# A CIN tower on one core: stream 1's first transfers move to ScalarE's queue, and gathers move ahead in GpSimd's

## The chip, the cores and the metric

The kernel runs on 1 core of one Trainium2 chip. Times are device microseconds (us) of one launch. A core has TensorE (PE in the profile), VectorE (DVE), ScalarE (ACT), GpSimd (POOL) and SyncE (SP, whose queue is SPq), and 16 DMA engines.

## The reference, cut to what matters

For each of 1024 samples, 32 rows of 16 numbers are looked up in 32 tables. Three layers multiply them with each other, and a small network follows.

```python
e = stack([tbl_f[ids[:, f]] for f in range(32)], axis=1)        # 1024 x 32 x 16
x0 = xk = e
for W in (W0, W1, W2):                                          # 32 x 32 x 64, then 32 x 64 x 64
    xk = relu(einsum('bmd,bhd,mhk->bkd', x0, xk, W))
    outs.append(sum(xk, axis=2))                                # 1024 x 64 each
h = concatenate([outs..., dense_ctx], axis=1)                   # 1024 x 208
h = maximum(h @ W_top1 + b_top1, 0); h = maximum(h @ W_top2 + b_top2, 0)
y = h @ W_top3
```

## The kernel before, in words

**Streams and tiles.** The 1024 samples are cut into 16 streams of 64. A stream's x0 has 64 x 16 = 1024 columns. Two streams, an even one (buffers a) and an odd one (b), make a tile, and the final network runs once per tile.

**Getting x0 in.** GpSimd looks up a stream's rows with 16 indirect DMAs (`gather`, L330), 256 in all, into `emb`, which has one half per stream of a tile. When a stream's 16 gathers have landed, SyncE stores `emb` twice to `x0_scratch` in HBM (`store_scratch`, L267), and then loads from there `base` (each field repeated on four partitions) and 16 chunks of `rolled` (`load_stream`, L285 and L294), 512 KB each: a chunk holds the fields turned by another number, so that all pairs of fields and maps come up. The first gather of stream i waits until stream i - 2 has been stored, since it overwrites its half of `emb`. SyncE goes through the streams one by one: the two stores, `base`, 16 chunks; for a stream above 1 each chunk waits until the stream two before has used its buffer.

**The layers.** A step is named (stream, layer, part). For each chunk an engine multiplies `rolled` with the layer's input, and TensorE multiplies the product with the chunk's weights and adds it up in `acc` (L591; in layer 0 also the squares, L600). The products are made by VectorE, two chunks at a time (`zd<-rolled`, L413, three buffers), and by GpSimd, one chunk at a time (`zg<-rolled`, L342, four buffers). VectorE reads the layer's input from PSUM (`xk_ps`), GpSimd from SBUF (`xk_sb`). Only in the very first step, (0,0,0), VectorE reads `base` from SBUF, chunk by chunk. At the end of layers 0 and 1 ScalarE copies `acc` with a ReLU to both inputs of the next layer (`evacuate`, L481), first `xk_sb`, then `xk_ps`, four halves each; only after (0,0) is part of the work done by VectorE (L422). At the start of a stream it copies `base` to `xk_ps` (L437) and squares it into `xk_sb` (L441).

**What sets the order.** `ORDER` lists the steps by hand: (0,0,0), (0,1,0), (1,0,0), (0,2,0), (1,1,0), (0,2,1), then tile by tile (1,2,0), (2,0,0), (1,2,1), (2,1,0), (3,0,0) and so on. `CHUNKS` says how many chunks of a step VectorE and GpSimd make. TensorE takes the products in the order of `merged`, VectorE's and GpSimd's interleaved.

**GpSimd's queue.** It holds gathers and products in one fixed order. `GATHERS_FIRST` gathers come first, then a wait for VectorE's first four products, then `GATHERS_EARLY` gathers; the two tables `GATHERS_AFTER` and `GATHERS_AFTER_AT` say how many gathers follow each product:

```python
gathers(GATHERS_FIRST)
pool.wait_ge(zd_ready, len(PLAN.dve[0]))
gathers(GATHERS_EARLY)
for q, (stream, layer, part) in enumerate(ORDER):
    ...
    for x, (_, n, j, _) in enumerate(PLAN.pool[q]):
        product(q, n, j)
        gathers(GATHERS_AFTER_AT.get(ORDER[q], GATHERS_AFTER.get((stream % 2, layer, part)))[x])
    gathers(GATHERS_MORE.get(ORDER[q], 0))
```

Of the kernel before, what the change touches and what calls it, by code (L numbers as in the profile page):

```python
# [15 lines left out]
FIELDS = 32  # L16
# [5 lines left out]
COLS = SAMPLES * DIM  # L22
# [7 lines left out]
GROUPS = P // FIELDS  # L30
GATHERS = SAMPLES // GROUPS
ROWS = 2 * FIELDS
NCH = FIELDS * MAPS // P
BASES = [1, 5, 9, 13, 0, 2, 3, 4, 6, 7, 8, 10, 11, 12, 14, 15]
L0CH = 4
# [4 lines left out]
ZD_BUFS = 3  # L40
ZG_BUFS = 4
# [10 lines left out]
for _t in range(1, TILES):  # L52
# [4 lines left out]
SUMS_AFTER = {0: 5, 1: 5, 2: 4}  # L57


GATHERS_FIRST = 24  # L60
GATHERS_EARLY = 8
GATHERS_AFTER = {(0, 1, 1): [3, 3], (1, 1, 0): [3, 3], (0, 2, 0): [3, 3, 2, 2], (1, 2, 0): [3], (1, 2, 1): [3, 4]}
GATHERS_AFTER_AT = {(0, 1, 0): [4, 7], (0, 2, 0): [3], (1, 1, 0): [3, 4], (0, 2, 1): [7],
                    (STREAMS - 1, 2, 0): [0, 0, 0, 0]}

GATHERS_MORE = {(2 * t, 1, 1): 3 for t in range(1, 6)}
# [34 lines left out]
PLAN = Plan()  # L101
# [50 lines left out]
def build_cin_tower(nc, ids, dense_t, tables, w0a, w0b, w12, wtop1, btop1, wtop2, btop2, wtop3, eye, out):  # L152
    with ExitStack() as ctx:
# [9 lines left out]
        rolled = sb("rolled", [P, 2, NCH, COLS])  # L163
# [86 lines left out]
        def bank_of(stream, layer):  # L250
            return 2 if layer == 0 else stream % 2

        def by_half(x):

            return x.rearrange("p (s h b) -> p s h b", s=2, h=2)
# [2 lines left out]
        last_h2_bank = [mlp[:, 0:TB], acc[:, 1, 0:TB]]  # L258
        last_y_bank = xk_ps[0:1, 0, 0:TB]

        @block.sync
        def _(sp):
            def store_scratch(i):

                sp.wait_ge(gathered[i % 2], 16 * GATHERS * (i // 2 + 1))
                for copy in range(2):
                    sp.dma_start(scratch[i, copy * FIELDS:(copy + 1) * FIELDS, :].rearrange(  # L267
                        "f (g c) -> (f g) c", g=GROUPS), emb[:, i % 2, :]).then_inc(scratch_in[i % 2], 16)

            def rows_from(first, i, step):  # L270
                return bass.AP(scratch.tensor, scratch.offset + (i * ROWS + first) * COLS,
                               [[COLS, FIELDS], [step * COLS, GROUPS], [1, COLS]])

            def load_stream(i):
                s = i % 2

                sp.wait_ge(scratch_in[s], 32 * (i // 2 + 1))
                if i > 0:

                    if i == 1:  # L280
                        sp.wait_ge(zd_ready, len(PLAN.dve[0]))
                    else:
                        sp.wait_ge(base_ps, 2 * (i - 1))
                    sp.wait_ge(squares_ready, i)
                sp.dma_start(base[:, :], rows_from(0, i, 0)).then_inc(base_in, 16)  # L285
                user = (i - 2, 2) if i > 1 else (i, 1)
                items = [x for q in range(len(ORDER)) if ORDER[q][:2] == user for x in PLAN.merged[q]]

                for who, n, first, w in sorted(items, key=lambda item: item[2] >= L0CH):
                    if i > 1:  # L290

                        sp.wait_ge(zd_ready if who == "dve" else zg_ready, n + 1)
                    for j in range(first, first + w):
                        sp.dma_start(rolled[:, s, j, :], rows_from(BASES[j], i, 1)).then_inc(rolled_in[s][j], 16)  # L294

            sp.dma_start(ids_sb[:, 0:1 + GATHERS], ids[:, 0:1 + GATHERS]).then_inc(first_ids_in, 16)
            sp.dma_start(ids_sb[:, 1 + GATHERS:], ids[:, 1 + GATHERS:]).then_inc(later_ids_in, 16)
            sp.dma_start(w0[:, :, :], w0a).then_inc(w0_in, 16)
            sp.dma_start(w0rev, w0b).then_inc(w0_in, 16)
            sp.dma_start(w12_sb[:, 0, :, :], w12[0]).then_inc(const_in, 16)  # L300
            sp.dma_start(w12_sb[:, 1, :, :], w12[1]).then_inc(const_in, 16)
            sp.dma_start(eye_sb[:, :], eye).then_inc(const_in, 16)
            sp.dma_start(wt1a[:, :], wtop1[0:P, :]).then_inc(const_in, 16)
            sp.dma_start(wt1b[:, :], wtop1[P:P + ZD_ROWS, :]).then_inc(const_in, 16)
            sp.dma_start(wt2[:, :, :], wtop2.rearrange("(c p) n -> p c n", p=P)).then_inc(const_in, 16)
            sp.dma_start(wt3[:, :], wtop3).then_inc(const_in, 16)
            sp.dma_start(bt1[:, :], btop1).then_inc(const_in, 16)
            sp.dma_start(bt2[:, :], btop2).then_inc(const_in, 16)
            sp.dma_start(z2d[MAPS:ZD_ROWS, :], dense_t).then_inc(const_in, 16)

            for i in range(STREAMS):
                store_scratch(i)
                load_stream(i)


            sp.wait_ge(y_ready, TILES)
            sp.dma_start(out.rearrange("b o -> o b"), y_sb[:, :]).then_inc(out_done, 16)
            sp.wait_ge(out_done, 16)
# [50 lines left out]
        def _(dve):  # L369
# [24 lines left out]
            for q, (stream, layer, _) in enumerate(ORDER):  # L394
                s = stream % 2
                if q == 0:

                    dve.wait_ge(base_in, 16)
                elif layer == 0:

                    dve.wait_ge(base_ps, 2 * stream)
                else:

                    dve.wait_ge(xk_ps_ready, 4 * evacuations(*phase_before(stream, layer)))
                for x, (_, n, j, w) in enumerate(PLAN.dve[q]):
                    if n >= ZD_BUFS:

                        dve.wait_ge(zd_used, n - ZD_BUFS + 1)
                    for c in range(j, j + w):
                        if layer == 0 or (layer == 1 and c >= L0CH):  # L410
                            dve.wait_ge(rolled_in[s][c], 16 * (stream // 2 + 1))
                    layer_in = base[:, :] if q == 0 else xk_ps[:, s, :]
                    nc.vector.tensor_tensor(zd[:, n % ZD_BUFS, 0:w, :], rolled[:, s, j:j + w, :],  # L413
                                            repeated(layer_in, w), ALU.mult).then_inc(zd_ready, 1)
                    for r in sums:
                        if sums[r] == (q, x):
                            reduce_d(r)
                if q == 0:

                    dve.wait_ge(zd_used, len(PLAN.dve[0]))  # L420
                    for copy in range(2):
                        nc.vector.tensor_scalar_max(xk_ps[copy * MAPS:(copy + 1) * MAPS, s, HALF:],  # L422
                                                    acc[MAPS:P, bank_of(0, 0), :], 0.0).then_inc(xk_ps_ready, 1)
# [5 lines left out]
        def _(act):  # L429
# [86 lines left out]
            act.wait_ge(base_in, 16)  # L516
            squares(0)
            evacuate(0, 0)
            base_to_ps(1)
            squares(1)  # L520
            evacuate(0, 1)
# [49 lines left out]
        def _(pe):  # L571
            def phase(q, between={}):
# [12 lines left out]
                for i, (who, n, j, w) in enumerate(merged):  # L585
                    pe.wait_ge(zd_ready if who == "dve" else zg_ready, n + 1)
                    for c in range(w):
                        weights = w0[:, j + c, :] if layer == 0 else w12_sb[:, layer - 1, j + c, :]
                        z = zd[:, n % ZD_BUFS, c, :] if who == "dve" else zg[:, n % ZG_BUFS, :]
                        for h in range(2):  # L590
                            end = nc.tensor.matmul(acc[h * MAPS:(h + 1) * MAPS, bank, :], weights,  # L591
                                                   z[:, h * HALF:(h + 1) * HALF],
# [154 lines left out]
```

## Time and profile before

| | |
|---|---|
| median of 3 runs | 616.87 us (615.1 to 616.98) |
| the profiled execution's own time | 617.09 us |
| its span in the profile | 615.3 us |
| TensorE busy | 562.9 us, 91% |
| VectorE busy | 553.3 us, 90% |
| GpSimd busy | 451.6 us, 73% |
| ScalarE busy | 366.7 us, 60% |
| DMA | 152.07 MB, mean 247 GB/s |
| chain that ended last | PE 74%, DVE 10%, DMA 6% |

The profile describes one execution. Busy time is the time in which an engine's instructions ran; a row's idle time stands in square brackets, with what ended it. The chain follows the last instruction back to what released it, step by step.

### The profile page before, as it was taken

The numbers are of one execution on the slowest core, as the hardware profiler recorded it, in microseconds if no ns is written. First come the engines' busy times: TensorE is split into PE (matmuls) and PEld (weight loads), VectorE is DVE, ScalarE is ACT, GpSimd is POOL, SyncE is SP. The second block draws the span as 40 slices with busy tenths as digits, with TensorE's granted clock in tenths as the row PEclk, the third lists the DMA queues.
The fourth block names the chain that finished last, engine by engine and source line by source line (L and its number), as shares of the span: only waits on it lengthen the run. The fifth ranks groups of instructions, "written<-read, shape, count | busy, mean of one in ns | idle before, by whom it ended". The sixth has DMA issues, their size and how long they took to land.

```text
span 615.3 us, 9070 instructions
## 1 busy us (share of the span) xinstructions
PE 562.9 (91%) x2752; PEld 209.7 (34%) x2752; DVE 553.3 (90%) x274; ACT 366.7 (60%) x2248; POOL 451.6 (73%) x347
## 2 busy tenths in 40 slices
PE   0049889999999999999999999999999999999997
PEld 0012222323333343334333333334333343334334
DVE  0058799999999999999999999999999999999990
ACT  0031606573867468774867468774868468674851
POOL 6748788878888788888888788888878864225430
PEclk9998899999999999999999999999999999999999
DMA  6297969793598819894598819794598809891000
GB/s 171 78 381 247 395 224 393 257 399 111 184 387 289 325 36 385 293 399 136 180 390 276 334 39 382 277 400 154 181 390 321 320 6 388 294 411 49 1 2 0
DMA packets 54259, 152.07 MB, mean 247 GB/s; under 512 B 9697, under 2 KB 18913, under 8 KB 54210
## 3 DMA queue, kind: packets, MB, share of 16 engines
q1 hardware_dynamic: 46018, 149.39, 64.6%
q0 software_dynamic: 8192, 2.11, 3.0%
q8 instruction: 21, 0.34, 0.2%
q14 instruction: 28, 0.23, 0.1%
HBM read 147.26 MB, written 4.20 MB: 246 GB/s over the span
## 4 chain that ended last, share of the span: by engine, by line
PE 74%; DVE 10%; DMA 6%; issue 4%; POOL 3%; SPq 1%; ACT 1%; DVEq 0%; POOLq 0%
PE acc L591 66%; DVE zd L413 10%; DMA rolled<-x_scratch 4%; POOL emb L330 3%; PE mlp L635 2%; PE acc L600 2%; PE mlp L626 1%; DMA emb<-tables_in,index 1%; PE mlp L627 1%; SPq L294 1%; DMA x_scratch<-emb 1%; PE mlp L607 1%; PE mlp L642 1%; ACT xk_sb L481 0%; ACT xk_ps L481 0%
## 5 line engine op out<-in xcount | busy, mean ns | idle before, releaser
L413 DVE TENSOR_TENSOR zd<-rolled,xk_ps 128x2048 f32<-128x2048 f32 (+1 forms) x246 | 536.1, 2254 | 11.6 <-DMA rolled<-x_scratch 5.3
L591 PE MATMUL acc<-zd,w_sb 128*64 128x512 f32 x1700 | 389.2, 596 | 8.9 <-DVE zd L413 8.8
L330 POOL DMA_INDIRECT emb<-tables_in,index x256 | 244.3, 954 | 79.6 <-issue 65.3
L342 POOL TENSOR_TENSOR zg<-rolled,xk_sb 128x1024 f32<-128x1024 f32 x87 | 207.1, 2383 | 59.3 <-ACT xk_sb L481 36.9
L591 PEld LDWEIGHTS acc<-zd,w_sb 128*64 128x64 f32 x1700 | 124.8, 137 | 250.2 <-issue 213.9
L460 ACT ACTIVATE relu_ab<-acc 128x16 f32<-128x16 f32 x928 | 153.7, 305 | 3.7 <-PE acc L591 3.5
L460 ACT ACTIVATION_READ_ACCUMULATOR relu_ab<-acc 128x1 f32 x928 | 154.3, 332 | 0.0
L481 ACT ACTIVATE xk_sb<-acc 64x512 f32<-64x512 f32 x128 | 75.8, 592 | 70.1 <-PE acc L591 67.5
L591 PE MATMUL acc<-zd,w 128*64 128x512 f32 x256 | 63.7, 618 | 38.6 <-DVE zd L413 38.6
L591 PE MATMUL acc<-zg,w_sb 128*64 128x512 f32 x348 | 90.7, 594 | 1.4 <-POOL zg L342 1.4
L481 ACT ACTIVATE xk_ps<-acc 64x512 f32<-64x512 f32 x126 | 71.8, 570 | 30.4 <-PE acc L591 27.6
L441 ACT ACTIVATE xk_sb<-base 128x1024 f32<-128x1024 f32 x16 | 16.9, 1057 | 57.0 <-PE acc L591 28.6
L591 PEld LDWEIGHTS acc<-zd,w 128*64 128x64 f32 x256 | 18.9, 142 | 74.2 <-issue 71.3
L591 PEld LDWEIGHTS acc<-zg,w_sb 128*64 128x64 f32 x348 | 25.3, 137 | 46.2 <-issue 42.9
L413 DVE TENSOR_TENSOR zd<-rolled,base 128x1024 f32<-128x1024 f32 x4 | 4.8, 1225 | 28.1 <-DMA rolled<-x_scratch 28.1
L437 ACT COPY xk_ps<-base 128x512 f32<-128x512 f32 x30 | 16.6, 587 | 22.3 <-DMA base<-x_scratch 17.8
L503 ACT ACTIVATE h<-mlp,bt 128x128 f32<-128x128 f32 x28 | 8.0, 368 | 23.8 <-PE mlp L627 23.8
L389 DVE TENSOR_REDUCE zpart<-relu_ab 128x32 f32<-128x512 f32 x19 | 13.0, 682 | 7.0 <-ACT relu_ab L493 7.0
L600 PE MATMUL acc<-xk_sb,w 128*64 128x512 f32 x64 | 18.4, 650 | 0.0
L497 ACT COPY z<-mlp 128x128 f32<-128x128 f32 x7 | 1.9, 266 | 24.0 <-PE mlp L607 20.6
L493 ACT ACTIVATE relu_ab<-acc 128x512 f32<-128x512 f32 x19 | 11.4, 598 | 7.5 <-PE acc L591 7.0
L635 PEld LDWEIGHTS mlp<-h,wt 128*128 128x128 f32 x112 | 13.0, 191 | 5.7 <-issue 5.7
(45 smaller groups left out, 102.5 us busy)
## 6 DMA issues: line engine op xcount, KB each, us to landing
rolled<-x_scratch SPq DMA_DIRECT2D x256, 512.0 KB, 10.3
base<-x_scratch SPq DMA_DIRECT2D x16, 512.0 KB, 3.7
emb<-tables_in,index POOLq DMA_INDIRECT x256
x_scratch<-emb SPq DMA_DIRECT2D x32, 128.0 KB
w_sb<-w_in SPq DMA_DIRECT2D x2, 512.0 KB, 5.0
wt<-wtop_in SPq DMA_DIRECT2D x1, 512.0 KB, 6.9
wt1a<-wtop_in SPq DMA_DIRECT2D x1, 256.0 KB, 5.8
w<-w0a_in SPq DMA_DIRECT2D x1, 160.0 KB, 2.3
```

What stands on the lines that cost most here:

```text
L330: pool.indirect_dma_start(emb[:, i % 2, c * DIM:(c + 1) * DIM], None, tables, bass.IndirectOffsetOnAxis(index[:, g:g + 1].bitcast(U32), 0) ...
L342: nc.gpsimd.tensor_tensor(zg[:, n % ZG_BUFS, :], rolled[:, s, j, :], xk_sb[:, s, :], ALU.mult).then_inc(zg_ready, 1)
L389: nc.vector.tensor_reduce(zpart[:, t % 2, layer, s, :], relu_ab[:, s, :].rearrange("p (b d) -> p b d", d=DIM), AX_X, ALU.add).then_inc(red ...
L413: nc.vector.tensor_tensor(zd[:, n % ZD_BUFS, 0:w, :], rolled[:, s, j:j + w, :], repeated(layer_in, w), ALU.mult).then_inc(zd_ready, 1)
L437: nc.scalar.copy(xk_ps[:, s, h * HALF:(h + 1) * HALF], base[:, h * HALF:(h + 1) * HALF]).then_inc(base_ps, 1)
L441: nc.scalar.activation(xk_sb[:, i % 2, :], base[:, :], ACT.Square).then_inc(squares_ready, 1)
L460: end = nc.scalar.activation(relu_ab[:, s, cols], acc[:, bank, cols], ACT.Relu, accum_out=zpart[:, t % 2, layer, s, b:b + 1])
L481: nc.scalar.activation(dst[copy * MAPS:(copy + 1) * MAPS, s, h * HALF:(h + 1) * HALF], acc[h * MAPS:(h + 1) * MAPS, bank, :], ACT.Relu).th ...
L493: nc.scalar.activation(relu_ab[:, s, :], acc[:, bank, :], ACT.Relu).then_inc(relu_ready, 1)
L591: end = nc.tensor.matmul(acc[h * MAPS:(h + 1) * MAPS, bank, :], weights, z[:, h * HALF:(h + 1) * HALF], start=(j + c == 0), stop=(i == len ...
L600: nc.tensor.matmul(acc[h * MAPS:(h + 1) * MAPS, bank, :], w0[:, L0CH, :], xk_sb[:, s, h * HALF:(h + 1) * HALF], start=False, stop=False)
L635: end = nc.tensor.matmul(mlp[:, c * TB:(c + 1) * TB], wt2[:, k, c * P:(c + 1) * P], h1[:, k, :], start=(k == 0), stop=(k == H1 // P - 1))
```

## The change

- The first tile's `GATHERS_FIRST` goes from 24 to 28 and `GATHERS_EARLY` from 8 to 4.
- The gathers behind GpSimd's first six products go from 4, 7, 3, 3, 4, 7 to 3, 2, 8, 5, 6, 8, four more in all, so that from there on every gather stands four places further ahead among the products.
- Stream 1's two stores, its `base` and its chunks 0 to 3 are issued by ScalarE, behind its evacuation of (0,0) and ahead of `base_to_ps(1)`, `squares(1)` and its evacuation of (0,1). SyncE keeps chunks 4 to 15 of stream 1, which wait for the same two stores.
- The first four products of VectorE go to both halves of two `zd` buffers, one chunk in each, and the wait for TensorE ahead of the fourth of them is gone.

```diff
-GATHERS_FIRST = 24
-GATHERS_EARLY = 8
+GATHERS_FIRST = 28
+GATHERS_EARLY = 4
...
-GATHERS_AFTER_AT = {(0, 1, 0): [4, 7], (0, 2, 0): [3], (1, 1, 0): [3, 4], (0, 2, 1): [7],
+GATHERS_AFTER_AT = {(0, 1, 0): [3, 2], (0, 2, 0): [8], (1, 1, 0): [5, 6], (0, 2, 1): [8],
...
+        def zd_of(q, n, w):
+
+            return zd[:, n // 2, n % 2:n % 2 + 1, :] if q == 0 else zd[:, n % ZD_BUFS, 0:w, :]
+
...
+        def load_chunk(engine, i, j):
+            engine.dma_start(rolled[:, i % 2, j, :], rows_from(BASES[j], i, 1)).then_inc(rolled_in[i % 2][j], 16)
...
-                sp.dma_start(base[:, :], rows_from(0, i, 0)).then_inc(base_in, 16)
+                if i != 1:
+                    sp.dma_start(base[:, :], rows_from(0, i, 0)).then_inc(base_in, 16)
...
-                        sp.dma_start(rolled[:, s, j, :], rows_from(BASES[j], i, 1)).then_inc(rolled_in[s][j], 16)
+                        if i != 1 or j >= L0CH:
+                            load_chunk(sp, i, j)
...
-                store_scratch(i)
+                if i != 1:
+                    store_scratch(sp, i)
...
-                    if n >= ZD_BUFS:
+                    if q > 0:
...
             evacuate(0, 0)
+
+            store_scratch(act, 1)
+            act.wait_ge(scratch_in[1], 32)
+
+            act.wait_ge(zd_ready, len(PLAN.dve[0]))
+            act.dma_start(base[:, :], rows_from(0, 1, 0)).then_inc(base_in, 16)
+            for j in range(L0CH):
+                load_chunk(act, 1, j)
             base_to_ps(1)
             squares(1)
             evacuate(0, 1)
```

GpSimd's queue from the start, before: gathers (`emb<-`) and products (`zg<-`), down to the product of (1,2,0), which is the seventh.

```order
L330 DMA emb<-tables_in,index 128x16 x32
...
L342 TENSOR_TENSOR zg<-rolled,xk_sb 128x1024
L330 DMA emb<-tables_in,index 128x16 x4
L342 TENSOR_TENSOR zg<-rolled,xk_sb 128x1024
L330 DMA emb<-tables_in,index 128x16 x7
L342 TENSOR_TENSOR zg<-rolled,xk_sb 128x1024
L330 DMA emb<-tables_in,index 128x16 x3
...
L330 DMA emb<-tables_in,index 128x16 x4
L342 TENSOR_TENSOR zg<-rolled,xk_sb 128x1024
L330 DMA emb<-tables_in,index 128x16 x7
```

The same piece now, with all six products and their gathers.

```order
L336 DMA emb<-tables_in,index 128x16 x32
...
L348 TENSOR_TENSOR zg<-rolled,xk_sb 128x1024
L336 DMA emb<-tables_in,index 128x16 x3
L348 TENSOR_TENSOR zg<-rolled,xk_sb 128x1024
L336 DMA emb<-tables_in,index 128x16 x2
L348 TENSOR_TENSOR zg<-rolled,xk_sb 128x1024
L336 DMA emb<-tables_in,index 128x16 x8
L348 TENSOR_TENSOR zg<-rolled,xk_sb 128x1024
L336 DMA emb<-tables_in,index 128x16 x5
L348 TENSOR_TENSOR zg<-rolled,xk_sb 128x1024
L336 DMA emb<-tables_in,index 128x16 x6
L348 TENSOR_TENSOR zg<-rolled,xk_sb 128x1024
L336 DMA emb<-tables_in,index 128x16 x8
```

The gathers are spread differently, and the seventh product stands behind 64 of them instead of 60.

ScalarE's queue now, from its evacuation of (0,0) to the one of (0,1).

```order
L499 ACTIVATE relu_ab<-acc 128x512
L273 DMA x_scratch<-emb 128x256 x2
L530 DMA base<-x_scratch 128x1x1024
L277 DMA rolled<-x_scratch 128x1x1024 x4
L443 COPY xk_ps<-base 128x512 x2
L447 ACTIVATE xk_sb<-base 128x1024
L487 ACTIVATE xk_sb<-acc 64x512 x4
L487 ACTIVATE xk_ps<-acc 64x512 x4
```

The three rows of DMAs are new there. On SyncE the row of stream 0's loads now reads x28 and runs on into stream 1's chunks 4 to 15.

## Rows read from the trace of the kernel before

**Rows 1.** Busy time by stretch: engines, then clock, DMA share, GB/s.

```profile
106.00:156.00 50.00, 47.71 (x230) 16.19 (x228) 49.85 (x26) 29.67 (x169) 41.89 (x33) 1.00 0.70 249
160.00:325.00 165.00, 165.00 (x816) 61.70 (x814) 163.90 (x80) 116.10 (x759) 142.28 (x109) 1.00 0.76 280
470.00:600.00 130.00, 130.00 (x662) 50.99 (x658) 127.39 (x61) 87.89 (x599) 65.64 (x35) 1.00 0.51 195
```

The engine columns are PE, PEld, DVE, ACT and POOL, each with its number of instructions.

**Rows 2.** Chain of waits, 20 to 90 us: start, length, what.

```profile
47.83 5.21 DMA emb<-tables_in,index
...
53.42 2.20 DMA x_scratch<-emb
...
56.84 6.77 DMA rolled<-x_scratch
```

**Rows 3.** Timeline of VectorE: start, length, operation, idle time before and what ended it.

```profile
55.07 4.48 DVE L413 TENSOR_TENSOR zd<-rolled,xk_ps 128x2048 f32<-128x2048 f32 x2
63.74 2.29 DVE L413 TENSOR_TENSOR zd<-rolled,xk_ps 128x2048 f32<-128x2048 f32 x1 [4.18 <-DMA rolled<-x_scratch]
66.49 8.88 DVE L413 TENSOR_TENSOR zd<-rolled,xk_ps 128x2048 f32<-128x2048 f32 x4 [0.47 <-DMA rolled<-x_scratch]
...
77.27 4.49 DVE L413 TENSOR_TENSOR zd<-rolled,xk_ps 128x2048 f32<-128x2048 f32 x2 [1.29 <-ACT xk_ps L481]
...
104.83 13.28 DVE L413 TENSOR_TENSOR zd<-rolled,xk_ps 128x2048 f32<-128x2048 f32 x6
```

**Rows 4.** Timeline of GpSimd: the gather after its stop, and four products.

```profile
39.09 0.94 POOL L330 DMA_INDIRECT emb<-tables_in,index  x1 [6.10 <-DVE zd L413]
...
48.87 2.39 POOL L342 TENSOR_TENSOR zg<-rolled,xk_sb 128x1024 f32<-128x1024 f32 x1
...
56.17 2.37 POOL L342 TENSOR_TENSOR zg<-rolled,xk_sb 128x1024 f32<-128x1024 f32 x1
...
67.18 2.37 POOL L342 TENSOR_TENSOR zg<-rolled,xk_sb 128x1024 f32<-128x1024 f32 x1
...
99.28 2.40 POOL L342 TENSOR_TENSOR zg<-rolled,xk_sb 128x1024 f32<-128x1024 f32 x1
```

**Rows 5.** Timeline of ScalarE, 59 to 68 us.

```profile
59.71 1.11 ACT L437 COPY xk_ps<-base 128x512 f32<-128x512 f32 x2 [13.56 <-DMA base<-x_scratch]
...
63.15 2.44 ACT L481 ACTIVATE xk_sb<-acc 64x512 f32<-64x512 f32 x4 [1.35 <-PE acc L591]
65.61 2.35 ACT L481 ACTIVATE xk_ps<-acc 64x512 f32<-64x512 f32 x4
```

**Rows 6.** Timeline of TensorE: its waits near 60 us, and step (1,2,0).

```profile
58.59 1.08 PE L591 MATMUL acc<-zg,w_sb 128*64 128x512 f32 x4 [1.41 <-POOL zg L342]
...
66.17 2.48 PE L591 MATMUL acc<-zd,w 128*64 128x512 f32 x8 [3.07 <-DVE zd L413]
...
104.47 1.94 PE L591 MATMUL acc<-zd,w_sb 128*64 128x512 f32 x8 [0.35 <-DVE zd L413]
106.21 1.06 PE L591 MATMUL acc<-zg,w_sb 128*64 128x512 f32 x4
```

**Rows 7.** Busy time by stretch around the second wait of rows 6.

```profile
64.00:68.00 4.00, 1.83 (x8) 0.87 (x10) 3.53 (x2) 3.83 (x8) 3.37 (x4) 0.93 1.03 400
68.00:72.00 4.00, 4.00 (x14) 1.42 (x12) 4.00 (x3) 0.59 (x1) 3.48 (x3) 0.65 1.04 395
```

**Rows 8.** Timelines of SyncE, GpSimd and TensorE, 449 to 469 us.

```profile
449.05 1.08 SPq L267 DMA_DIRECT2D x_scratch<-emb  x2
...
453.98 2.40 POOL L342 TENSOR_TENSOR zg<-rolled,xk_sb 128x1024 f32<-128x1024 f32 x1
...
462.39 0.94 POOL L330 DMA_INDIRECT emb<-tables_in,index  x1 [3.62 <-DMA x_scratch<-emb]
463.34 2.40 POOL L342 TENSOR_TENSOR zg<-rolled,xk_sb 128x1024 f32<-128x1024 f32 x1
...
463.84 1.03 PE L591 MATMUL acc<-zg,w_sb 128*64 128x512 f32 x4
...
468.13 1.03 PE L591 MATMUL acc<-zg,w_sb 128*64 128x512 f32 x4
```

More of the change, by code:

```diff
@@ L259, in build_cin_tower, with rows_from, store_scratch @@
         last_y_bank = xk_ps[0:1, 0, 0:TB]
+        def rows_from(first, i, step):
+            return bass.AP(scratch.tensor, scratch.offset + (i * ROWS + first) * COLS,
+                           [[COLS, FIELDS], [step * COLS, GROUPS], [1, COLS]])
+        def store_scratch(engine, i):
+            engine.wait_ge(gathered[i % 2], 16 * GATHERS * (i // 2 + 1))
+            for copy in range(2):
+                engine.dma_start(scratch[i, copy * FIELDS:(copy + 1) * FIELDS, :].rearrange(
+                    "f (g c) -> (f g) c", g=GROUPS), emb[:, i % 2, :]).then_inc(scratch_in[i % 2], 16)
+        def load_chunk(engine, i, j):
+            engine.dma_start(rolled[:, i % 2, j, :], rows_from(BASES[j], i, 1)).then_inc(rolled_in[i % 2][j], 16)
         @block.sync
         def _(sp):
[L263 to L272, printed above, removed]
-            def load_stream(i):
[L275 to L283, printed above, removed]
+            def load_stream(i):
+                sp.wait_ge(scratch_in[i % 2], 32 * (i // 2 + 1))
+                if i > 1:
+                    sp.wait_ge(base_ps, 2 * (i - 1))
                     sp.wait_ge(squares_ready, i)
-                sp.dma_start(base[:, :], rows_from(0, i, 0)).then_inc(base_in, 16)
+                if i != 1:
+                    sp.dma_start(base[:, :], rows_from(0, i, 0)).then_inc(base_in, 16)
                 user = (i - 2, 2) if i > 1 else (i, 1)
@@ L412, in _ @@
                     layer_in = base[:, :] if q == 0 else xk_ps[:, s, :]
-                    nc.vector.tensor_tensor(zd[:, n % ZD_BUFS, 0:w, :], rolled[:, s, j:j + w, :],
+                    nc.vector.tensor_tensor(zd_of(q, n, w), rolled[:, s, j:j + w, :],
                                             repeated(layer_in, w), ALU.mult).then_inc(zd_ready, 1)
@@ L588, in phase @@
                         weights = w0[:, j + c, :] if layer == 0 else w12_sb[:, layer - 1, j + c, :]
-                        z = zd[:, n % ZD_BUFS, c, :] if who == "dve" else zg[:, n % ZG_BUFS, :]
+                        z = zd_of(q, n, w)[:, c, :] if who == "dve" else zg[:, n % ZG_BUFS, :]
                         for h in range(2):
```

## The prediction, made before the changed kernel was run

> **What bounds the kernel now.** I read four views in this order: busy time by stretch, the chain of waits, the timelines of the engines in the first 110 us, and those around 450 us.
>
> Busy time by stretch splits the run in three [rows 1]. From 160 us on TensorE has no idle time: 165.00 of 165 us, 130.00 of 130 us between 470 and 600. Whatever makes it wait there lengthens the run by as much. Between 106 and 156 us VectorE is busy 49.85 of 50 us and TensorE 47.71: VectorE sets the pace, and TensorE could take back some 2.3 us. Ahead of that lie the waits that the change is aimed at. The chain has them one behind the other [rows 2]: stream 1's last gather, issued at 47.83 and landed 5.21 us later, its store (2.20), and the loads that land at 63.61. VectorE pays 4.18 us at 63.74, 0.47 at 66.49 and 1.29 at 77.27 [rows 3], 5.9 us in all: the most that the change can win.
>
> **The front, stream 1.** The four gathers that move ahead of GpSimd's stop fit into its 6.10 us of idle time [rows 4]. After the stop four remain, so the last is issued at 39.09 + 3 x 1.25 = 42.84 instead of 47.83 and lands at 48.05 if it takes 5.21 again. ScalarE then issues the store. If that lands as before, 2.58 us after the gather, it is there at 50.6; if it takes the 5.21 of the gather beside the loads of stream 0, at 53.3; before, at 55.62. From there VectorE's first product of stream 1 came 8.1 us later, its second 10.9 later, the base's copy on ScalarE 4.1 [rows 3, 5]. What the trace of before doesn't show is two queues loading at once: SyncE issues stream 1's other 12 chunks from the same semaphore on. Lower bound: they cost nothing. Upper bound: they take half of the rate, so base, chunk 0 and 1 need 3 x 1.3 us more and chunks 2 and 3 another 2 x 1.3 (512 KB at the 395 GB/s of a loaded stretch is 1.3 us [rows 7]). The first product starts at 58.7 to 65.3, the second at 61.5 to 70.7, against 63.74 and 66.49. The gathers, which suffered beside loads (5.21 us), are the nearest row, so I take sharing, with the early store: 62.6 and 68.0.
>
> The Trainium skill, "DMA: Bandwidth & Descriptors", section "Issuing engines are not separate DMA queues", says that transfers issued by different engines run on the same 16 DMA engines and interleave, and that only the sequencer's issue time is saved. By that rule the split gains nothing in bandwidth and takes some from the first chunks; the trace of before has no two such queues to show it.
>
> A second limit stands behind the loads. VectorE's next phase, (0,2,0), reads xk_ps of (0,1). Its last product for (0,1) ends at 59.55 [rows 3], TensorE takes 1.94 for a pair of chunks [rows 6], and ScalarE copies xk_sb in 2.44 and then xk_ps in 2.35 [rows 5]: 61.6, 64.1, 66.4. The 1.41 us that TensorE waits for GpSimd's second product [rows 6] go, since that product starts earlier, and this is included. So (0,2,0) starts at 66.4 at best and at 73.0 at worst, before at 68.7; with my values at 70.2. Three products and a sum (7.3 us: before 68.7 to 77.27 less the wait of 1.29) bring (1,1,0) to 73.7, 80.3 or 77.5; before it began at 77.27. **The front is worth -3.6 to +3.0 us to VectorE; I take 0.** ScalarE waits for the base in between; even at 50.6 + 4.1 + 1.3 = 56.0, or 53.3 + 5.4 = 58.7, it has 2.2 us of copying to do before 61.6, so that costs nothing as long as the base has landed by 59.4.
>
> The second buffer half for the first four products (the removed wait) is worth nothing: they wait for their chunks, not for TensorE. Their cover is the loading of stream 0.
>
> **GpSimd, where the price is.** From product to product it takes 7.30 us with 4 gathers between (48.87 to 56.17) and 11.01 with 7 (56.17 to 67.18) [rows 4]: 2.35 + 1.24 per gather. Before, the gathers behind its first six products were 4, 7, 3, 3, 4, 7; now 3, 2, 8, 5, 6, 8. The first two of these fall in a time where it then has to wait: its third product, of (0,2,0), needs xk_sb of (0,1), which is there at 64.1, as worked out. This was 67.18 before, behind seven gathers. From 64.1 on nothing lets GpSimd pause: 8 gathers, product at 76.4; 5, 84.9; 6, 94.7; 8, the product of (1,2,0) at 107.0, ended at 109.4. Each of these is behind its gathers alone: xk_sb of (1,0), the only other thing that one of them needs anew, is there by 75. Before it began at 99.28 and TensorE took it at 106.21 [rows 4, 6]. **TensorE has to wait there until 109.4, 3.2 us later than before**, however early VectorE is. VectorE has three buffers, so it goes on at first. The product of 104.83 is the next that TensorE takes, and its buffer serves the third one after it, which started at 104.83 + 3 x 2.2 = 111.4 [rows 3]. Now TensorE frees it after GpSimd's chunk and that pair of chunks (1.06 and 1.94, which overlap by 0.2 [rows 6]), at 109.4 + 2.8 = 112.2. So 0.8 us stay with VectorE, and the rest TensorE takes back by 156. But an idle TensorE loses its clock: after an idle time of 3.07 us the granted clock was 0.93 and then 0.65 over two stretches of 4 us [rows 6, 7], from 2.4 GHz to 1.2 GHz for part of them, a loss of 4 x 0.07 + 4 x 0.35 = 1.7 us. Here it idles for 3.2 us if VectorE is on time, more if it is early. So 0.8 to 2.5 (the drop delays the same buffer); the idle time lies close to the one that brought the drop, and I take a value between, 1.8.
>
> **The same queue, 340 us later.** Gather 240, stream 15's first, waits for the store of stream 13, whose buffer it overwrites. That store was issued at 449.05, behind 16 loads in SyncE's queue, and released GpSimd at 462.39 after 3.62 us of waiting [rows 8]. Gather 240 was the third behind the product of 453.98, and the product of 463.34 came right after. With all gathers four further on, gather 240 stands ahead of the product of 453.98, with one more gather between. Even 5 us late GpSimd reaches it before 459, so it waits for the store as before, and now the product of 453.98 stands behind it: 462.39 + 1.25 + 0.95 = 464.6, ended 467.0, where TensorE took it at 463.84: 3.1 us of waiting. The next product is due at 464.6 + 2.35 + 3 x 1.24 = 470.7, ended 473.1, taken at 468.13 before: 4.9 us in all, on top of the shift that the tile already has. TensorE has no idle time there to take it back [rows 1]. A clock drop at the first of the two waits only moves time from the second.
>
> **Sum.** 0 (front) + 1.8 + 4.9 = 6.7 us on the profiled execution's 617.09, that is 623.8; the median of the runs shown is 0.2 lower, so 623.6.
>
> **Rivals.**
> - *The second wait does not come* (12%): the store of stream 13 lands earlier relative to TensorE, or gather 240 is not behind it. Against it: the order of the queue and 3.62 us of waiting already there. Only 1.8 us are left: 618.7, on the edge of what counts as no change.
> - *The front gain gets through* (6%), the faster side. It decides at TensorE's wait at 106.21: if GpSimd's products of the first tile went out of its queue 4 us sooner than 2.35 + 1.24 per gather allows, so that the one of (1,2,0) ended by 105, the 3.6 us would stay: 613.3. It needs the wait at 462.39 to be harmless as well.
> - *ScalarE is held* (10%). Its store, base and loads stand ahead of its evacuation of (0,1). If the base lands at 63 instead of by 59.4, xk_sb, GpSimd's third product and all behind it slip by 3.6: 627.2.
> - *The early gathers and the first products collide* (8%). Four gathers now run beside VectorE's first four products, which read two SBUF tensors; before, GpSimd stood still there. If each held a product up for its 0.94 us, everything slips by 3.8: 627.4. The Trainium skill, "SBUF — State Buffer", section "SBUF: two separate sides", says that GpSimd and a VectorE instruction with two SBUF inputs lock each other out of a shared port pair; no row of before has the two together.
>
> **Chances.** Forecast 64%, rivals 12, 6, 10 and 8%. A measurement can tell 0.3% (1.85 us) from no change: faster than 615.0 has 6%, within it 11%, slower 83%. The range reaches from the first rival (618.6) to just over the dearest (628.0); it leaves out the faster side and sums of two misfortunes.
>
> **What would show it.** In the profile after, GpSimd's product of (1,2,0) should end near 109.4, and TensorE should show a wait for it of 2 to 6 us, against none before. Near 465 to 473 us (plus 2) there should be two waits of TensorE for zg, with GpSimd waiting for x_scratch a product earlier. VectorE's waits of 4.18 and 1.29 should be smaller or moved. It is wrong if TensorE never waits for zg past 100 us, if the third GpSimd product starts before 63, or if stream 1's base lands after 60.

## The result, and the profile after

The changed kernel takes 624.75 us (median of 6 runs, 623.83 to 627.11), the kernel before, in turn with it on the same chip, 616.65 (6 runs, 614.52 to 617.14). The ratio is 1.0135, with a 95% interval from 1.0105 to 1.0164: 8.1 us slower, with 6.5 to 10.1 as the interval. The forecast was 623.6, the range 618.6 to 628.0.

TensorE after 100 us first. The waits by engine, of the changed kernel, TensorE's rows (engine, line, operand, releaser: us in total, times, longest):

```profile
PE acc L605 <- DVE zd L419: 50.0, 18, 35.5
PE acc L605 <- POOL zg L348: 5.5, 5, 1.6
```

Five waits for GpSimd's product (zg), 5.5 us. Past 100 us the kernel before had none. Their places are in the timeline of TensorE, changed kernel:

```profile
110.81 1.08 PE L605 MATMUL acc<-zg,w_sb 128*64 128x512 f32 x4 [1.34 <-POOL zg L348]
...
449.66 1.03 PE L605 MATMUL acc<-zg,w_sb 128*64 128x512 f32 x4
450.52 1.89 PE L605 MATMUL acc<-zd,w_sb 128*64 128x512 f32 x8
453.97 1.08 PE L605 MATMUL acc<-zg,w_sb 128*64 128x512 f32 x4 [1.56 <-POOL zg L348]
...
458.77 1.08 PE L605 MATMUL acc<-zg,w_sb 128*64 128x512 f32 x4 [0.28 <-POOL zg L348]
...
470.06 1.08 PE L605 MATMUL acc<-zg,w_sb 128*64 128x512 f32 x4 [0.78 <-POOL zg L348]
...
476.09 1.08 PE L605 MATMUL acc<-zg,w_sb 128*64 128x512 f32 x4 [1.51 <-POOL zg L348]
```

The chunks that TensorE took at 106.21, 463.84 and 468.13 [rows 6, 8] it now takes at 110.81, 470.06 and 476.09. The shift is 4.60 at the first and 7.96 at the last. Two more chunks, matched by their place in the order of steps, tell when it grows: the one taken at 157.24 before is taken at 160.30, the one at 446.68 at 449.66. So the shift is 3.0 us at 160 and still 3.0 at 450; the rest of the first 4.60 was taken back. **The 8 us are two losses: 3.0 that are there by 160, and 5.0 between 449.66 and 476.09.**

The first loss starts at VectorE. Its timeline, changed kernel:

```profile
55.98 4.47 DVE L419 TENSOR_TENSOR zd<-rolled,xk_ps 128x2048 f32<-128x2048 f32 x2
65.83 2.29 DVE L419 TENSOR_TENSOR zd<-rolled,xk_ps 128x2048 f32<-128x2048 f32 x1 [5.38 <-DMA rolled<-x_scratch]
70.95 8.88 DVE L419 TENSOR_TENSOR zd<-rolled,xk_ps 128x2048 f32<-128x2048 f32 x4 [2.83 <-DMA rolled<-x_scratch]
...
80.35 4.47 DVE L419 TENSOR_TENSOR zd<-rolled,xk_ps 128x2048 f32<-128x2048 f32 x2
```

The wait of 1.29 us for xk_ps before (1,1,0) [rows 3] is gone, but those for the loads have grown from 4.18 and 0.47 to 5.38 and 2.83, and (1,1,0) begins at 80.35 instead of 77.27: 3.1 us late. ScalarE's timeline says when these loads could start:

```profile
48.88 0.83 ACTq L273 DMA_DIRECT2D x_scratch<-emb  x2
54.80 0.60 ACTq L530 DMA_DIRECT2D base<-x_scratch  x1
55.43 2.91 ACTq L277 DMA_DIRECT2D rolled<-x_scratch  x4
60.36 1.11 ACT L443 COPY xk_ps<-base 128x512 f32<-128x512 f32 x2 [13.32 <-DMA base<-x_scratch]
61.41 1.05 ACT L447 ACTIVATE xk_sb<-base 128x1024 f32<-128x1024 f32 x1
62.49 2.44 ACT L487 ACTIVATE xk_sb<-acc 64x512 f32<-64x512 f32 x4
```

The store is issued at 48.88, and the base, which waits for it, at 54.80: 5.9 us. It was issued 4.2 us earlier than before and landed only 0.8 earlier, at 54.78 against 55.62. Until shortly before that stream 0's loads fill the DMA engines (386 to 403 GB/s from 40 to 52 us). From 54.80 two queues load. By the landings in the trace ScalarE's chunks 0 to 3 come at 63.15, 65.71, 68.27 and 70.83, each 2.56 us after the other, with a chunk of SyncE's between each two (65.39, 67.95, 70.51). Before, chunks 0 to 3 came at 61.97, 63.61, 64.89 and 66.37, 1.3 to 1.6 us apart.

GpSimd's timeline, changed kernel, first tile:

```profile
33.12 0.94 POOL L336 DMA_INDIRECT emb<-tables_in,index  x1 [0.30 <-issue]
34.36 1.82 POOL L336 DMA_INDIRECT emb<-tables_in,index  x1 [0.30 <-issue]
36.48 1.02 POOL L336 DMA_INDIRECT emb<-tables_in,index  x1 [0.30 <-issue]
37.81 1.12 POOL L336 DMA_INDIRECT emb<-tables_in,index  x1 [0.30 <-issue]
39.76 0.94 POOL L336 DMA_INDIRECT emb<-tables_in,index  x1 [0.83 <-DVE zd L419]
...
65.00 2.35 POOL L348 TENSOR_TENSOR zg<-rolled,xk_sb 128x1024 f32<-128x1024 f32 x1 [7.72 <-ACT xk_sb L487]
...
108.38 2.37 POOL L348 TENSOR_TENSOR zg<-rolled,xk_sb 128x1024 f32<-128x1024 f32 x1
```

The third product is early (65.00, before 67.18), the one of (1,2,0) late (108.38, before 99.28). The 27 gathers between them are the cause, with one wait of 0.58 us at 77.79, for the xk_sb of (1,0), which ScalarE had ready at 77.72.

Around 460 us, GpSimd's timeline of the changed kernel:

```profile
456.31 2.40 POOL L348 TENSOR_TENSOR zg<-rolled,xk_sb 128x1024 f32<-128x1024 f32 x1
458.87 0.98 POOL L336 DMA_INDIRECT emb<-tables_in,index  x1 [0.16 <-issue]
465.43 0.94 POOL L336 DMA_INDIRECT emb<-tables_in,index  x1 [5.58 <-DMA x_scratch<-emb]
466.67 0.94 POOL L336 DMA_INDIRECT emb<-tables_in,index  x1 [0.30 <-issue]
467.64 2.37 POOL L348 TENSOR_TENSOR zg<-rolled,xk_sb 128x1024 f32<-128x1024 f32 x1
...
473.67 2.36 POOL L348 TENSOR_TENSOR zg<-rolled,xk_sb 128x1024 f32<-128x1024 f32 x1
```

Gather 240 is held at the store of stream 13 for 5.58 us (before 3.62 [rows 8]); this wait is called the hold from here on. It ends at 465.43, and behind gather 240 comes one more gather before the product of 467.64.

### The profile page after: what moved, and what is told of

The parts are those of the page before. It is cut to its first block, busy times and chain, and to the rows that moved or that the text cites. A ratio compares the mean times of both kernels' runs of the same rounds, so it can differ in the third digit from the quotient of the medians.

```text
span 623.2 us, 9069 instructions
## 1 busy us (share of the span) xinstructions
PE 564.2 (91%) x2752; PEld 207.8 (33%) x2752; DVE 553.9 (89%) x274; ACT 365.7 (59%) x2248; POOL 452.7 (73%) x347
## 4 chain that ended last, share of the span: by engine, by line
PE 63%; POOL 19%; issue 8%; DMA 5%; DVE 3%; SPq 1%; ACT 1%; DVEq 0%; POOLq 0%
PE acc L605 56%; POOL emb L336 13%; POOL zg L348 7%; DMA rolled<-x_scratch 2%; DMA x_scratch<-emb 2%; DVE zd L419 2%; PE mlp L649 2%; PE acc L614 2%; PE mlp L640 1%; PE mlp L641 1%; SPq L277 1%; PE mlp L656 1%; PE mlp L621 1%; DMA emb<-tables_in,index 0%; ACT xk_sb L487 0%
```

## The experiments

Theory A, from the two traces: the change has two independent costs. The queue split brings the front in 3 to 4 us late, and the four gathers that GpSimd is ahead move the hold at gather 240 in front of a product, for 5. GpSimd's late product of (1,2,0) is a third limit, hidden while VectorE is late itself. Rival B: one cause, GpSimd's gathers, makes all of it, and the front is only jitter. Rival C: the queue split costs by itself whatever the loads do (ScalarE's issues ahead of its copies). Each experiment's recorded expectation stands ahead of its result and may name further rivals. Differences are taken against the kernel before as timed beside each (616.46 for the first four, 616.06 for the next four).

**1. The queue alone.** The change with the gather numbers of before:

```diff
-GATHERS_FIRST = 28
-GATHERS_EARLY = 4
+GATHERS_FIRST = 24
+GATHERS_EARLY = 8
-GATHERS_AFTER_AT = {(0, 1, 0): [3, 2], (0, 2, 0): [8], (1, 1, 0): [5, 6], (0, 2, 1): [8],
+GATHERS_AFTER_AT = {(0, 1, 0): [4, 7], (0, 2, 0): [3], (1, 1, 0): [3, 4], (0, 2, 1): [7],
```

> The queue part alone: ScalarE issues stream 1's stores, base and first four chunks, GpSimd's order of gathers is the one before the change. Theory A (two separate costs: 3 us because two queues share the engines at stream 1's first chunks, and 5 us because gather 240 stands ahead of the product that TensorE takes at 464; together 8): the store lands near 55.6, chunks 2 and 3 then need 16 us as after the change, so VectorE's step (1,1,0) starts near 81 instead of 77.3 and the kernel is 3 to 4 us slower than before, 620 to 621, with no wait of TensorE for zg near 465. Theory B (all comes from GpSimd being four gathers late): no change, 616.7. Theory C (ScalarE is held by its transfers): its evacuation of (0,1) starts later than 63.2 and the cost grows with it.

Measured 620.25 us, ratio 1.0065 [1.0049, 1.0082]: 3.8 us slower. VectorE, this kernel:

```profile
65.36 2.29 DVE L419 TENSOR_TENSOR zd<-rolled,xk_ps 128x2048 f32<-128x2048 f32 x1 [7.46 <-DMA rolled<-x_scratch]
70.86 8.88 DVE L419 TENSOR_TENSOR zd<-rolled,xk_ps 128x2048 f32<-128x2048 f32 x4 [3.22 <-DMA rolled<-x_scratch]
...
80.26 4.47 DVE L419 TENSOR_TENSOR zd<-rolled,xk_ps 128x2048 f32<-128x2048 f32 x2
```

These are the starts of the change itself within 0.5 us, with GpSimd's gathers as before. B falls. The run also holds the new `zd` halves of the first four products, which no run has alone; in the trace of before the fourth of them waited only for its chunk (0.19 us, at 37.60), not for TensorE.

**2. The gathers alone.** The kernel before, all loads on SyncE, with the change's gather numbers (28 and 4; [3, 2], [8], [5, 6], [8]).

> The gathers part alone, all of stream 1's transfers on SyncE as before. Theory A: no sharing of two queues, so VectorE's step (1,1,0) starts 1 to 2 us earlier than before (75 to 76), but GpSimd's product of (1,2,0) ends near 110.7 whatever VectorE does, TensorE waits for it by 3 us or more, and 2 to 4 us stay; near 465 the same 5 us as after the change. 624 to 626, as slow as the whole change. Theory B agrees. Theory D (the sharing of the queues is the cause of the front's 3 us and GpSimd's lateness there costs nothing): only the 5 us near 465 less what the front gains, 620 to 621.

Measured 623.29 us, ratio 1.0129 [1.0096, 1.0162]: 6.8 slower, a little less than expected. (1,1,0) begins at 75.47, 1.8 earlier than before, and TensorE waits 2.81 us for the product of (1,2,0). At the chunk of 157.24 1.1 of the 1.8 are left, and at the one of 446.68, taken at 445.79 here, 0.9; between them lies one more wait for GpSimd, 0.29 us at 176.38. The waits near 450 to 472 are there as in the change: from that chunk to the one of 468.13 it is 26.66 us. By the medians the two halves alone cost 3.8 + 6.8 = 10.6 and together 8.1. That is no proof of an overlap: the interval of this run reaches from 5.9 to 10.0 us (its four times from 621.53 to 626.93), and the traces, read at the chunk of 468.13, give 2.3 (experiment 1), 4.3 (this run, its fastest execution) and 8.0 (the change).

**3. The hold moved back.** The change with three gathers fewer behind step (10,1,1), in the tile of streams 10 and 11. Gather 240 then stands one place ahead of where it stood before the change, not four, and behind the same product as there:

```diff
-GATHERS_MORE = {(2 * t, 1, 1): 3 for t in range(1, 6)}
+GATHERS_MORE = {(2 * t, 1, 1): 3 for t in range(1, 5)}
```

> The changed kernel with three gathers fewer in tile 5 (behind stream 10's second part of layer 1), so that gather 240 stands behind the product that TensorE takes at 464 to 467 and not ahead of it. Theory A: the two waits of TensorE for zg near 467 and 473 are gone and so are the small ones ahead of them; 5 us less than the change, 619.5 to 620.5. Theory B' (GpSimd as a whole is the bound by then, and the hold only shows it): it stays within 1 us of the change, 624.

Measured 619.75 us, ratio 1.0047 [1.0030, 1.0064]. That is 3.3 us slower than before: three gathers less in one place give back 4.8 of the 8.1. TensorE and GpSimd, this kernel:

```profile
449.83 1.03 PE L605 MATMUL acc<-zg,w_sb 128*64 128x512 f32 x4
...
467.00 1.03 PE L605 MATMUL acc<-zg,w_sb 128*64 128x512 f32 x4
...
471.29 1.03 PE L605 MATMUL acc<-zg,w_sb 128*64 128x512 f32 x4
```

```profile
458.62 2.38 POOL L348 TENSOR_TENSOR zg<-rolled,xk_sb 128x1024 f32<-128x1024 f32 x1
...
465.62 0.94 POOL L336 DMA_INDIRECT emb<-tables_in,index  x1 [3.48 <-DMA x_scratch<-emb]
...
467.83 2.39 POOL L348 TENSOR_TENSOR zg<-rolled,xk_sb 128x1024 f32<-128x1024 f32 x1
```

The hold ends at the same time, 465.62 against 465.43, though SyncE issued the store that ends it 3.6 us earlier here (452.16 against 455.79). But the product of 458.62 is now ahead of it and TensorE takes that one at 467.00 without a wait. 449.83 to 471.29 is 21.46 us, as before the change (446.68 to 468.13, 21.45); in the change it is 26.43.

**4. The hold alone, in the kernel before.** One line, nothing else of the change. Gather 240 comes to stand three places further ahead, directly in front of a product:

```diff
+GATHERS_MORE[10, 1, 1] = 6
```

> The kernel before with three gathers more behind tile 5's second part of layer 1, so that gather 240 stands ahead of the product that TensorE takes at 464; nothing else. Theory A: the hold by the store of stream 13 costs alone what it costs in the change, TensorE waits near 464 and 468 for zg, 5 us in all, 621 to 622. Rival (the hold costs only with GpSimd already late from the first tile): under 1 us, 616.5 to 617.5.

Measured 620.50 us, ratio 1.0073 [1.0058, 1.0087]: 4.4 slower, somewhat under expectation. From 445.86 to 470.88 TensorE takes 25.02 us for what took 21.45, so this trace has 3.6 of it. GpSimd, this kernel:

```profile
461.47 0.94 POOL L331 DMA_INDIRECT emb<-tables_in,index  x1 [5.79 <-DMA x_scratch<-emb]
462.43 2.37 POOL L343 TENSOR_TENSOR zg<-rolled,xk_sb 128x1024 f32<-128x1024 f32 x1
...
468.46 2.37 POOL L343 TENSOR_TENSOR zg<-rolled,xk_sb 128x1024 f32<-128x1024 f32 x1
```

The hold alone makes the larger part of the change's loss in a kernel that is otherwise the one before. The change loses 1.4 more there, and its trace says why: the product for TensorE's last wait starts 8.24 us after the end of the hold (465.43 to 473.67), here 6.99 (461.47 to 468.46). The difference, 1.25, is the one gather more that four places instead of three put between them.

**5. SyncE lets ScalarE's loads go first.** The change, with SyncE's chunks 4 to 15 of stream 1 behind the landing of chunk 3:

```diff
                 if i != 1:
                     sp.dma_start(base[:, :], rows_from(0, i, 0)).then_inc(base_in, 16)
+                else:
+                    sp.wait_ge(rolled_in[1][L0CH - 1], 16)
```

> The changed kernel, but SyncE starts its 12 chunks of stream 1 only when ScalarE's four have landed. Theory A: with the engines to themselves chunks 2 and 3 land near 65 instead of 70.8, VectorE's (1,1,0) starts near 75 instead of 80.4; but GpSimd's product of (1,2,0) still ends near 110.7, TensorE waits for it 3 to 7 us, loses clock, and 2 to 4 us stay behind it. With the 5 us near 465 it comes out at 623 to 626, no better than the change. Theory D (sharing alone is the front's cost, GpSimd's lateness is harmless): 3 to 5.5 us less than the change, 619 to 621.5.

Measured 624.04 us, ratio 1.0129 [1.0098, 1.0160]: 7.6 slower, against 8.1 for the change. (1,1,0) begins at 75.38 instead of 80.35, so the 3 us of the front come from sharing the DMA engines, not from ScalarE's queue as such: C falls. And the median hardly moves. A part of the reason is in TensorE's timeline, this kernel:

```profile
107.75 1.08 PE L607 MATMUL acc<-zg,w_sb 128*64 128x512 f32 x4 [3.23 <-POOL zg L350]
108.66 3.28 PE L607 MATMUL acc<-zd,w_sb 128*64 128x512 f32 x8
```

GpSimd's late product takes over as the limit, and the clock drops. (1,1,0) began 1.9 us earlier than before, but the chunk of 446.68 is taken at 447.08, 0.4 later: this wait took 2.3 us, where the one of experiment 2, without a drop, took 0.9. From there to the chunk of 468.13 it is 26.50 us, so the hold is 5.05. That makes 5.5 us, and the trace does have 2.6 of the 3.0 us of the front back. The rest of the 7.6 it doesn't show: the four times fall in two pairs, 622.21 and 622.56, 625.52 and 625.77. The trace is of the execution at 622.56, 2.5 faster than the profiled one of the change (625.05); of the slower pair there is none.

**6. Gathers refitted.** The change with the numbers behind the first products set so that gather 240, and the product of (1,2,0), stand as before:

```diff
-GATHERS_AFTER_AT = {(0, 1, 0): [3, 2], (0, 2, 0): [8], (1, 1, 0): [5, 6], (0, 2, 1): [8],
+GATHERS_AFTER_AT = {(0, 1, 0): [3, 8], (0, 2, 0): [3], (1, 1, 0): [3, 4], (0, 2, 1): [7],
```

> The changed kernel's queues, but the gathers behind the six products 3, 8, 3, 3, 4, 7: 28 of them as before the change, eight of them in the time in which GpSimd waits for xk_sb of (0,1). Theory A: GpSimd's product of (1,2,0) ends near 98 to 100, TensorE waits for no zg after 60 us, nothing is lost near 465, and what is left is the sharing of the two queues at stream 1: VectorE's (1,1,0) near 80 as after the change, 3 to 4 us slower than before, 619.5 to 620.5. Rival (queues harmless, all of the cost in the gathers' order): 616 to 617.

Measured 620.40 us, ratio 1.0059 [1.0045, 1.0074]. TensorE has no wait for zg at all, so all GpSimd costs are gone, and 4.3 us stay: the shared loads, as in 1.

**7. Both.** Experiments 5 and 6 together.

> As the last, and SyncE holds its 12 chunks of stream 1 back until ScalarE's four have landed: no sharing, no late GpSimd, no hold ahead of the product. Theory A: both costs are gone. The front gives no more than 0.3 us, as the run with SyncE waiting showed (its store landed no earlier, behind the loads of stream 0). 616 to 617, no change from before. Rival (a third cost, such as ScalarE's transfers or the early gathers beside the first products, is still in it): 618 or more.

Measured 615.46 us (12 runs), ratio 0.9984 [0.9974, 0.9995]: 0.6 faster than the kernel before, and 9 faster than the change. With the two causes away, none of the 8 us is left. VectorE, this kernel:

```profile
62.03 9.12 DVE L421 TENSOR_TENSOR zd<-rolled,xk_ps 128x2048 f32<-128x2048 f32 x4 [3.19 <-DMA rolled<-x_scratch]
...
76.83 4.49 DVE L421 TENSOR_TENSOR zd<-rolled,xk_ps 128x2048 f32<-128x2048 f32 x2 [1.97 <-ACT xk_ps L489]
```

The first product comes 1.7 us earlier than before [rows 3], but (1,1,0) only 0.4: VectorE waits 0.84 us for TensorE at 71.98 and 1.97 for the copy into xk_ps, the next limit.

**8. The copies swapped.** Experiment 7, and ScalarE copies xk_ps ahead of xk_sb after (1,0):

```diff
-                    if (s, layer) != (0, 0):
+                    if (s, layer) != (0, 0) and (stream, layer) != (1, 0):
                         copies.reverse()
```

> As the run with refitted gathers and SyncE waiting, and ScalarE copies xk_ps before xk_sb after (1,0), since VectorE waits 1.3 to 1.5 us there for xk_ps while GpSimd's next product has over 9 us of slack. Theory A: VectorE's wait at its step (1,1,0) goes, 1.3 us less than that run, about 615.3. Rival (VectorE's lead is lost again before TensorE becomes the bound at 150 us, since GpSimd's products come 2.4 us later): no gain, 616.5.

Measured 614.60 us (8 runs, 613.39 to 618.31), ratio 0.9983 [0.9966, 0.9999]. VectorE, this kernel:

```profile
64.13 8.88 DVE L421 TENSOR_TENSOR zd<-rolled,xk_ps 128x2048 f32<-128x2048 f32 x4 [0.35 <-DMA rolled<-x_scratch]
...
73.52 4.47 DVE L421 TENSOR_TENSOR zd<-rolled,xk_ps 128x2048 f32<-128x2048 f32 x2
```

The wait is gone and (1,1,0) begins 3.8 us earlier than before. It is the fastest median of the study, 1.5 us under the kernel before, with an interval that just stays below 1. Whether it beats experiment 7 these runs do not say.

**9 and 10. The first wait alone; one queue.** Two questions were left: what the late product of (1,2,0) costs without the hold (experiment 5 with the line of experiment 3), and whether the best version needs ScalarE's queue at all (the kernel before with 28 and 4, [3, 8], [3], [3, 4], [7] and the copies swapped). Each ran in two series.

> The changed kernel with both other costs taken out: SyncE waits for ScalarE's four chunks, and tile 5 has three gathers fewer. What is left is GpSimd's lateness in the first tile, 64 gathers ahead of its product of (1,2,0). Theory A: that product ends near 107.7, TensorE waits 2.8 to 3.3 us for it and 1.8 to 2.6 us stay: 618 to 619. Rival (a wait of TensorE in a stretch paced by VectorE is taken back whole): 615.5 to 616.5.

> The kernel before, with 28 gathers ahead of the stop, 3 and 8 behind the first two products, and xk_ps copied before xk_sb after (1,0); all transfers on SyncE. Theory A (ScalarE's queue gives nothing, since the store waits for the loads of stream 0 in whichever queue it stands): as fast as the run with the copies swapped, 614.6, within 0.5 us. Rival (the second queue brings the store earlier and this is where the gain of the last two runs came from): 616 or more.

> The same kernel as in the run of the first wait alone, whose step (0,1) began 7 us late (at 50.1) beside a before whose runs spread over 6 us. Theory (the late product of (1,2,0) is a floor of its own, worth some 2 us when the front is on time): step (0,1) begins near 42 to 43.5, VectorE's (1,1,0) at 75.5, TensorE waits about 3.2 us for zg near 105 to 108, no wait for zg near 450 to 475; 618 to 619, ratio to before 1.003 to 1.004. Rival (the two floors are one and the same loss, so that without the second the first costs nothing): 616. Second rival (the late step belongs to this kernel and not to its surroundings): step (0,1) again at 50, some 5 us over before.

> The same kernel as in the run of one queue with the earlier gathers and the copies swapped, whose step (0,1) also began at 50.0. Theory (the second queue has no part in the gain of the best version: it comes from the gathers ahead of GpSimd's stop and from xk_ps being copied first): step (0,1) near 42 to 43.5, VectorE's (1,1,0) near 73.5, no wait for zg past 100 us, 614.6, ratio 0.997 to 0.999. Rival (ScalarE's queue gives a part of it): 615.5 to 616, ratio 0.999 to 1.000. Second rival (the late step belongs to this kernel): step (0,1) again at 50, some 5 us over before.

Measured: the first wait alone 627.40 and 627.43 us (ratios 1.0105 [1.0058, 1.0153] and 1.0148 [1.0086, 1.0211]); one queue 626.37 and 624.54 (1.0084 [1.0042, 1.0126] and 1.0101 [1.0073, 1.0128]). All are far off, and not by a mechanism that the first two expectations asked about; the last two name it as their second rival. ScalarE, in the first of them:

```profile
48.60 1.17 ACT L489 ACTIVATE xk_ps<-acc 64x512 f32<-64x512 f32 x2 [17.53 <-remote]
```

In all four profiles the first evacuation, (0,0), starts between 48.28 and 48.60 us, where the change has it at 42.9 and the other kernels between 39.4 and 42.5. TensorE, VectorE and ScalarE stand still from 44 to 48, while the DMA engines go on, and TensorE's granted clock is 0.50 in the stretch after. TensorE's last matmuls were issued by 41 in all of them; what held their results isn't in the trace. SyncE is late as well: it issues the last chunk of stream 0 between 43.3 and 44.2 us, in the other kernels between 37.0 and 38.2.

The second rival of the last two expectations, that the late step belongs to these kernels, came about as far as it can be seen: (0,1) began at 49.76 and 49.88 again, and the two kernels were 9.6 and 6.8 us over before. Each run of the new kernels is over 621. But the kernel of the first wait alone does the same as that of experiment 5 until step (10,1,1), near 415 us, and there (0,1) began at 41.86, so the order of its work up to there isn't enough to cause it. And in these two series the kernel before itself spread over 614.6 to 623.3 us, which it did in no other, so the surroundings have a part. The cause stays open, and with it both questions. What the first wait costs is known only from what it leaves of an earlier front: 0.9 in the trace of experiment 2 and 2.3 in that of experiment 5.

## Why the prediction was right

Right in direction, in size (1.2 us off, inside the range) and in its largest term. One term was wrong by +3.1, and one of 1.8 was added where it should not have been. That the two offset each other in part was luck: the total is off by less than either of these terms.

- **The front, taken as 0: wrong, it was +3.1**, the upper end that the prediction worked out (80.3; measured 80.35). The step that failed is "I take sharing, with the early store". Sharing came. The early store did not: it landed 5.9 us after its issue, not the 2.58 that were taken, and more than the 5.21 of the bound (53.3; measured 54.78). Its nearest row was the gather beside the loads of stream 0, which the prediction had in hand and used only as a bound. With it the sum had been right for the front, though by two errors that cancel: the store was 1.5 us later than the bound, and from it to the first two products it took 11.05 and 16.17 us, 2.9 and 5.3 more than before, where half of the rate was worked out as 3.9 and 6.5.
- **The rule of the Trainium skill** ("DMA: Bandwidth & Descriptors", "Issuing engines are not separate DMA queues") speaks of transfers of two issuers interleaving on the same 16 DMA engines. The trace agrees: 2.56 us per chunk of 512 KB on ScalarE's queue beside SyncE's, against 1.3 to 1.6 alone, one of each in turn.
- **The product of (1,2,0): right in place, its cost hidden.** It was to end at 109.4 and ended at 110.75: GpSimd's third product began at 65.00 and not at 64.1, and at 77.79 it waited 0.58 us for the xk_sb of (1,0), which the prediction had "there by 75" and which the late front moved to 77.72. TensorE waited 1.34 us for it and not 3.2: VectorE was late itself. The 1.8 us of the sum were not there: the shift, 3.1 at the chunk before it (99.55), is 4.6 at 106.21 and 3.1 again at 137.03, and experiment 3 repeats it (3.0, 4.5, 3.0, with a wait of 1.36). With the front on time the waits were 2.81 us without a drop of the clock and 3.23 with one. They cost 0.7 and 2.7 us at the chunk of 157.24, 0.9 and 2.3 at the one of 446.68 (experiments 2 and 5; shifts drift by up to 0.7 between these two chunks with no wait for zg, as in experiment 1): about the two ends of the 0.8 to 2.5, each with the cause that the prediction gave for it. The slower executions of both kernels have no trace. What failed is the addition: the late front and the late product are two limits in parallel, the later one rules, and a front that is 3 us late doesn't pay for the product as well.
- **The hold at gather 240: right.** Taken 4.9; measured 4.98 in the trace (26.43 less 21.45), 4.8 by experiment 3, 5.2 and 5.05 in the traces of experiments 2 and 5, 3.6 in the kernel before with three places instead of four (experiment 4; 4.4 by its times), where the one gather fewer behind the hold makes 1.25 of the difference. The product that was to start at 464.6 and the next at 470.7, with the tile's shift of 3.0, started at 467.64 and 473.67. Only the waits lie differently: four of 0.28 to 1.56 us from 453.97 on, not two. The first two come from products that GpSimd made ahead of the hold, which holds it from 459.85 on: it was late there already. They add nothing to the 5.0, since the last product starts 8.24 us after the end of the hold in any case (the same in experiments 2 and 5).
- **The sum.** 0 + 1.8 + 4.9 = 6.7 forecast; 3.1 + 0 + 5.0 = 8.1 measured.
- **The rivals.** "The second wait does not come": it did. "The front gain gets through": there was none. "ScalarE is held": the base landed at 60.34, past the 59.4 set for it, and ScalarE's copy of (0,1) began at 62.49 instead of 61.6. No run shows that the base caused these 0.9 us: TensorE ended (0,1) at 62.44 and ScalarE its work on the base at 62.46, and (0,1) had begun 0.9 us later than before (44.38 against 43.48, in the traces of the eight other kernels that ran as expected 40.85 to 43.98). It cost nothing in the end. The late base was also on the list of what would make the prediction wrong ("lands after 60"): by that sign it should have been wrong, and what the sign tells of is the late store, the step that failed. "The early gathers and the first products collide": they do, but the other way round. The gathers took 1.82, 1.02 and 1.12 us instead of 0.94, while VectorE's products took 1.22 to 1.23 each, as before. GpSimd had 6 us to spare there, so it cost nothing. That agrees with the Trainium skill, "SBUF — State Buffer", "SBUF: two separate sides", as far as one locks out the other. The Trainium skill says there that whichever starts first has the shared ports for its whole instruction. The gather of 34.36, begun 0.22 us after a product, fits that; those of 36.48 and 37.81 began ahead of the products of 36.89 and 38.27, and still it was they that took longer.

## What to carry to other kernels

A second queue is no second path: issuing the urgent transfers there helps only if the others are held back meanwhile (5.0 us at the start of (1,1,0), from one wait on SyncE), and a store issued 4 to 5 us early lands only 0.8 to 1.8 us earlier while the DMA engines are full (54.78 in the change, 53.8 in experiments 2 and 5, 55.62 before). Where one engine does both background work and products in a fixed order, count where the background work can be held (here gather 240), and what stands right behind it: moving it by four places in the first tile cost 5 us some 400 us later, and one line takes them back. Limits that run in parallel are not added: work out when each would release the pacing engine, take the latest, and expect the next one to appear when it is removed.

## What the runs showed of the hardware

- **The clock after an idle time.** TensorE idled 2.81 us in experiment 2 and kept the upper of its two levels (2.4 GHz); 3.23 us in experiment 5, and it fell towards 1.2 GHz, as after the 3.07 us in the kernel before [rows 6, 7]. The stretches 108 to 112 of the two, the granted clock the third number from the end:

```profile
108.00:112.00 4.00, 4.00 (x22) 1.33 (x20) 3.38 (x2) 0.67 (x9) 3.38 (x4) 1.00 0.61 202
```

```profile
108.00:112.00 4.00, 4.00 (x14) 1.26 (x12) 1.62 (x1) 0.59 (x8) 3.37 (x4) 0.62 1.02 398
```

 The pair of chunks after the wait took 1.89 us in the one and 3.28 in the other. The length of the idle time alone doesn't decide: in experiment 8 the clock was 0.62 from 64 to 68 us after an idle time of 2.82, and in experiment 7 it stayed at 1.00 from 44 to 52 around one of 3.86 that ended at 45.12.
- **A stop of TensorE costs more than its wait.** The chunks from 449.66 to 476.09 took 4.98 us longer, with 4.13 us of waiting in the rows. Without a stop an operation starts 0.17 us before the end of the one ahead (449.66 + 1.03 against 450.52), after one it doesn't, and it takes 1.08 instead of 1.03: 0.22 for each of four stops, 0.9 in all.
- **A small transfer behind full DMA engines.** The store of 256 KB took 5.9 us from issue to landing while stream 0 was loading, against 2.58 (53.05 to 55.63) in the kernel before, where it was issued as that load ended. A queue of its own made no difference: in experiment 2 it went through SyncE's and took 5.1 (48.72 to 53.83). The store of stream 13 shows the same behind 16 loads in SyncE's own queue: issued 3.6 us apart in the change and in experiment 3 (455.79 and 452.16), it released the base behind it at 465.18 and 465.38.
